# A graph-attention and mixture-of-experts kernel: dense edge stage on chip from counted node pairs

## The chip, the cores and the metric

The kernel runs on one core of one Trainium2 chip. The metric is the device time of one execution in microseconds, here the median of three runs.

## What is computed

x has 2500 nodes of 512 features, and 40000 edges (src, dst) come sorted by dst. Everything is fp32.

```python
h = layernorm(x) @ W + b_w
e = leaky_relu((h @ a[:512])[dst] + (h @ a[512:])[src] + b_a, 0.2)
w = exp(e)
alpha = w / segment_sum(w, dst)[dst]
x = x + segment_sum(alpha[:, None] * h[src], dst)
n = layernorm(x)
probs = softmax(n @ Wg + bg)
x = x + sum over the top 2 of 8 experts of probs_e * (gelu(n @ W1[e] + b1[e]) @ W2[e] + b2[e])
```

Since the weight of an edge depends on its two nodes alone, edges that join the same pair have the same weight.

## The kernel before, in words

The nodes lie in NT = 20 tiles of 128, the edges in 313 chunks of 128, four chunks to a group (GC = 4), 79 groups.

**Node rows.** For a pair of tiles u, ACT rounds the transposed x (`high_xT`, L867), POOL takes the rest (L496), PE multiplies the two halves with the two halves of the centred W (`products`, L645, 12 products a tile), DVE scales, adds the bias and takes the two dot products with a (`node_rows`, L1089, L1096), ACT turns these into scores (`scores`, L885, L888) and SP stores the rows in `node_table` in DRAM (L394). `ps_d` (L678) spreads the scores of the destinations along the free axis.

**Edges.** POOL gathers one row per edge from `node_table` with an indirect DMA per chunk (`gather`, L508) into a ring of eight groups. For each group ACT makes both exponentials of the leaky relu against a window of 128 destinations (`weights`, L915); DVE takes the larger (`largest`, L1150) and masks it with the edge's destination (`masked`, L1162); PE multiplies the result with the rows (`sums`, L686); DVE adds the sums into `acc` for the window (`add`, L1171). A word per group says where its window lies and whether it needs further ones (`extras`). POOL's order is the gathers' order; DVE's is mask of group g, then add of group g-2.

**Second normalisation and logits**, after the last group: for a pair of tiles DVE divides, adds x (`x1_of`, L1274) and takes statistics (L1280, L1287), ACT the root and the normalised rows (L951, L961), PE transposes (`normal_T`, L727), multiplies with Wg (`logits`, L736) and turns back (`logits_of_nodes`, L743), ACT copies between (L969, L976). SP stores x and the normalised rows, then loads W2 and W1 (L442, L436).

**Routing and experts**: DVE ranks the items, with one-hots in bf16 (L1383 to L1417), PE counts (L785, L794), and tiles of 128 routed items go through the experts with a gather (L595) and an adding scatter (L604) each. The change leaves these alone but for the rows that count as valid.

## Time and profile before

| what | us |
|---|---|
| timed runs, median of 3 (lowest, highest) | 771.3 (770.13, 773.55) |
| the profiled execution, first to last instruction | 843.5 |
| its PE, DVE, ACT, POOL busy | 630.6, 456.8, 356.8, 478.4 |

The profiled execution is one execution; its own time is known as its span alone, and that is 72.2 us above the median of the timed runs. Busy time of PE counts its matmul records; an fp32 product leaves two records, one of fp32r or bf16 one.

### The profile page before, as it was taken

The numbers are of one execution on the slowest core, as the hardware profiler recorded it, in microseconds if no ns is written. First come the engines' busy times: TensorE is split into PE (matmuls) and PEld (weight loads), VectorE is DVE, ScalarE is ACT, GpSimd is POOL, SyncE is SP. The second block draws the span as 40 slices with busy tenths as digits, with TensorE's granted clock in tenths as the row PEclk, the third lists the DMA queues.
The fourth block names the chain that finished last, engine by engine and source line by source line (L and its number), as shares of the span: only waits on it lengthen the run. The fifth ranks groups of instructions, "written<-read, shape, count | busy, mean of one in ns | idle before, by whom it ended". The sixth has DMA issues, their size and how long they took to land.

```text
span 843.5 us, 13398 instructions
## 1 busy us (share of the span) xinstructions
PE 630.6 (75%) x2874; PEld 497.9 (59%) x2875; DVE 456.8 (54%) x1139; ACT 356.8 (42%) x956; POOL 478.4 (57%) x550
## 2 busy tenths in 40 slices
PE   4997335766676757766686667774988899999992
PEld 2886224655564646655565555662645787888881
DVE  3999224564555546645555655579758433333331
ACT  3232323343443434433443434335864444545551
POOL 4461775666665666656666566501104377777773
PEclk9999677989999998798979889995998999999997
DMA  9482675656666656666666666505897277777765
GB/s 310 154 286 103 179 211 146 194 166 178 186 177 174 187 168 189 175 183 167 185 184 182 169 179 189 164 2 188 306 352 285 66 136 133 137 135 134 138 117 71
DMA packets 59260, 147.26 MB, mean 175 GB/s; under 512 B 8965, under 2 KB 18437, under 8 KB 58968
## 3 DMA queue, kind: packets, MB, share of 16 engines
q0 software_dynamic: 35216, 106.84, 50.3%
q1 hardware_dynamic: 24008, 40.01, 13.7%
q8 instruction: 14, 0.23, 0.1%
q14 instruction: 22, 0.18, 0.1%
HBM read 118.46 MB, written 28.35 MB: 174 GB/s over the span
## 4 chain that ended last, share of the span: by engine, by line
PE 45%; DVE 21%; issue 14%; DVEq 7%; another core or an unknown queue 6%; DMA 3%; SPq 1%; ACT 1%; POOLq 0%; POOL 0%; ACTq 0%
PE ps L686 22%; PE ps L825 8%; PE ps L839 6%; DVE acc L1171 4%; DVE S L1162 4%; DVE Wt L1150 3%; DVE junk L1096 3%; PE ps L736 2%; PE ps L815 2%; DVE rows L1089 1%; DMA x_all<-in_x_dram 1%; DVEq L1202 1%; DVEq L1171 1%; PE ps L727 1%
## 5 line engine op out<-in xcount | busy, mean ns | idle before, releaser
L686 PE MATMUL ps<-rows,S 128*128 128x257 f32 x1252 | 325.9, 423 | 156.9 <-DVE acc L1171 107.1
L508 POOL DMA_INDIRECT rows<-node_table,srcT x313 | 298.4, 953 | 178.5 <-issue 86.7
L686 PEld LDWEIGHTS ps<-rows,S 128*128 128x128 f32 x1252 | 263.1, 214 | 219.5 <-issue 160.7
L915 ACT ACTIVATE E<-sdst_w,rows 128x128 f32 x313 | 100.1, 390 | 284.0 <-DVE Wt L1150 187.7
L1171 DVE TENSOR_TENSOR acc<-acc,ps 64x514 f32 x160 | 110.1, 688 | 147.8 <-PE ps L686 68.6
L1162 DVE SCALAR_TENSOR_TENSOR S<-ps,lane,Wt 128x128 f32<-128x128 f32 x313 | 88.2, 345 | 26.3 <-issue 13.9
L915 ACT ACTIVATE ps<-sdst_w,rows 128x128 f32 x313 | 96.0, 350 | 0.0
L825 PE MATMUL ps<-W_e,xgT 128*128 x352 | 83.4, 380 | 0.0
L604 POOL DMA_INDIRECT out_dram<-y,si x44 | 70.4, 1601 | 12.1 <-issue 6.3
L825 PEld LDWEIGHTS ps<-W_e,xgT 128*128 128x128 f32 x352 | 63.4, 190 | 6.9
L645 PE MATMUL ps<-Wb,xT 128*128 128x512 f32 x240 | 56.5, 398 | 6.0 <-DVE Wb L1108 5.0
L839 PE MATMUL ps<-W_hi,hidT 128*128 x176 | 55.4, 437 | 3.8 <-DVE hidT L1452 3.7
L1469 DVE TENSOR_TENSOR y_b<-ps,b_b 128x512 f32<-128x512 f32 x44 | 30.4, 692 | 47.9 <-PE ps L839 36.8
L645 PEld LDWEIGHTS ps<-Wb,xT 128*128 128x128 f32 x240 | 46.0, 193 | 16.6 <-DVE Wb L1108 5.8
L1150 DVE SCALAR_TENSOR_TENSOR Wt<-E,ps 128x512 f32<-128x512 f32 (+1 forms) x79 | 53.0, 671 | 0.0
L595 POOL DMA_INDIRECT xg<-xn_table,gi x44 | 48.1, 1094 | 7.9 <-issue 5.1
L1022 ACT ACTIVATE act_h<-hid 128x256 f32<-128x256 f32 x44 | 18.4, 418 | 75.7 <-DVE hid L1459 66.9
L1459 DVE TENSOR_TENSOR hid<-ps,b_b 128x256 f32<-128x256 f32 x44 | 18.7, 424 | 51.1 <-PE ps L825 49.8
L496 POOL TENSOR_TENSOR xT<-xf,xT 128x1024 fp32r<-128x1024 f32 x10 | 26.2, 2616 | 29.0 <-ACT xT L867 29.0
L1155 DVE TENSOR_TENSOR lane<-dstT,base 128x4 f32 (+1 forms) x79 | 12.8, 162 | 54.4 <-issue 51.4
L553 POOL COPY si<-dst_row 128x1 int32 (+1 forms) x45 | 31.0, 689 | 18.9 <-DVE need L1443 11.3
L839 PEld LDWEIGHTS ps<-W_hi,hidT 128*128 128x128 f32 x176 | 32.5, 189 | 13.3 <-issue 7.7
(202 smaller groups left out, 612.9 us busy)
## 6 DMA issues: line engine op xcount, KB each, us to landing
W_e<-in_L_ffn_W_dram SPq DMA_DIRECT2D x16, 512.0 KB, 8.9
node_table<-rows SPq DMA_DIRECT2D x20, 258.0 KB, 3.2
xf<-in_x_cols_dram SPq DMA_DIRECT2D x10, 512.0 KB, 6.1
out_dram<-acc SPq DMA_DIRECT2D x20, 256.0 KB, 2.6
xn_table<-xn SPq DMA_DIRECT2D x20, 256.0 KB, 2.4
rows<-node_table,srcT POOLq DMA_INDIRECT x313
x_all<-in_x_dram SPq DMA_DIRECT2D x19, 256.0 KB, 6.6
b_b<-in_L_ffn_b_dram SPq DMA_DIRECT2D x1, 2048.0 KB, 14.6
```

The costliest lines, as they stand in the source:

```text
L508: nc.gpsimd.indirect_dma_start(out=rows[:, g % RING, c, :], out_offset=None, in_=table, in_offset=bass.IndirectOffsetOnAxis(ap=srcT[:, GC ...
L553: nc.gpsimd.tensor_copy(si[:, r, :], dst_row[:, bass.ds(i, 1)]).then_inc(si_ok, 1)
L595: nc.gpsimd.indirect_dma_start(out=xg[:, r, :], out_offset=None, in_=xn_table, in_offset=bass.IndirectOffsetOnAxis(ap=gi[:, r, :], axis=0) ...
L604: nc.gpsimd.indirect_dma_start(out=result, out_offset=bass.IndirectOffsetOnAxis(ap=si[:, (r - LAG) % YR, :], axis=0), in_=y[:, (r - LAG) % ...
L645: m = pe.matmul(ps_h[s][j][:, :], xT[:, s, a, k, j * P:(j + 1) * P], Wb[:, b, k, :], start=(n == 0), stop=(n == 3 * KT - 1))
L686: m = pe.matmul(ps_agg[q][:, a, 0:HALF], S[:, w, c, :], rows[:, r, c, a * HALF:(a + 1) * HALF], start=(c == 0), stop=(c == n - 1))
L825: m = pe.matmul(ps_hid[1 - s][:, 0:F], xgT[:, 1 - s, k * P:(k + 1) * P], W1_e[:, bass.ds(e, 1), k, :].rearrange("p e f -> p (e f)"), start ...
L839: m = pe.matmul(ps_y[s][:, :], hidT[:, s, a, k * P:(k + 1) * P], W[:, bass.ds(e, 1), k, :].rearrange("p e d -> p (e d)"), start=(c == 0), ...
L915: m = nc.scalar.activation(e[:, c, :], sdst_w[:, bass.ds(w, 1), :].rearrange("p w n -> p (w n)"), ACT.Exp, bias=bias, scale=scale)
L1150: return nc.vector.scalar_tensor_tensor(out=Wt[:, q, 0:n, :], in0=E1[:, q, 0:n, :], scalar=FINITE, in1=(E2x[:, 0, 0:n, :] if q == 2 else p ...
L1162: m = nc.vector.scalar_tensor_tensor(out=S[:, k, c, :], in0=ps_id[:, bass.ds(turn_of, P)], scalar=lane[:, k, c:c + 1], in1=Wt[:, q, c, :], ...
L1171: m = nc.vector.tensor_tensor(a, a, ps_agg[q][part, :, 0:HALF], ALU.add)
```

## The change

The tiles now hold TN = 125 nodes each (20 x 125 = 2500), padded to 128 rows. The rows h stay on chip, as a rounded half `H_hi` and the rest `H_lo`; `node_table` and all its gathers go. For a tile t of destinations the kernel counts how many edges join each pair of source and destination: the source is written as (tile k, place), and for ten half banks of 250 columns (12.5 destinations by 20 source tiles) PE multiplies a one-hot of the sources' places (`hot_l`) with a one-hot of (destination, source tile) (`hot_k`), both bf16, three chunks of edges for each half. A table of words says at which chunk each half begins; where three chunks do not do, a loop of extras follows. ACT makes the weight of every pair of the tile (20 relus and 20 exponentials of 128 x 125, one for each source tile), DVE multiplies it with the counts (`weigh`), sums it over the source tiles as a tree (`fold`), and splits it; PE multiplies it with H in three terms (hi hi, hi lo, lo hi), 60 products of 512 columns. x plus the sum, its statistics, the root (by POOL, in Newton steps from a seed), the normalised rows, their transposes and the logits are made inside the same loop, one to three tiles behind.

```diff
-    table = nc.dram_tensor("node_table", [NTN, ROW], F32).ap()
-            def gather(g):
-...
-                    nc.gpsimd.indirect_dma_start(
-                        out=rows[:, g % RING, c, :], out_offset=None, in_=table,
-                        in_offset=bass.IndirectOffsetOnAxis(ap=srcT[:, GC * g + c:GC * g + c + 1], axis=0))\
+        def over_node_tiles(eng, step, first=-1):
+
+            for t in range(first, 4):
+                step(t, t % 2)
+            with eng.Fori(2, NT // 2 - 1) as i:
+                for s in range(2):
+                    step(2 * i + s, s)
+            for t in range(NT - 2, NT + 3):
+                step(t, t % 2)
# POOL
+            def low_rows(u, s):
+                for j in range(2):
+                    pool.wait_ge(H_hi_ok, 2 * u + j + 1)
+...
+                    nc.gpsimd.tensor_tensor(H_lo[:, 2 * u + j, :], hrow[:, s, j, :],
+                                            H_hi[:, 2 * u + j, :].bitcast(F32), ALU.subtract).then_inc(H_lo_ok, 1)
+            def rstd_of_tile(t, s):
+...
+                after(nc.gpsimd.tensor_scalar(low, v, -0.5, None, ALU.mult), 1)
+                for n in range(3):
+                    after(nc.gpsimd.tensor_scalar(part, y, y, low, ALU.mult, ALU.mult), 2 * n + 2)
+                    if n < 2:
+                        after(nc.gpsimd.tensor_scalar(y, part, 1.5, y, ALU.add, ALU.mult), 2 * n + 3)
# PE
+            def count(t):
+...
+                if not (isinstance(t, int) and t < 1):
+                    pe.wait_ge(A_ok, t)
+                for h in range(HALVES):
+                    pe.wait_ge(pairs_ok, HALVES * t + h + 1)
+                    for c in range(BASE - h % 2):
+                        pe.matmul(half_of(h), low_of(h, c), hot_k[:, BASE * h + c, :],
+                                  start=(h % 2 == 0 and c == 0), stop=False)
+...
+            def tile_products(t, s):
+
+                if has(t, -1):
+                    count(t + 1)
+                if has(t, 0):
+                    if not (isinstance(t, int) and t < 1):
+                        pe.wait_ge(x1_ok, t)
+                    for k in range(NT):
+                        if k % (NT // 4) == 0:
+                            pe.wait_ge(A_hi_ok, 4 * t + k // (NT // 4) + 1)
+                        pe.matmul(ps_agg[0:TN, :], A_hi[:, k, :], H_hi[:, k, :], start=(k == 0), stop=False)
+                        m = pe.matmul(ps_agg[0:TN, :], A_hi[:, k, :], H_lo[:, k, :], start=False, stop=False)
+...
+                    for k in range(NT):
+                        if k % (NT // 4) == 0:
+                            pe.wait_ge(A_lo_ok, 4 * t + k // (NT // 4) + 1)
+                        m = pe.matmul(ps_agg[0:TN, :], A_lo[:, k, :], H_hi[:, k, :], start=False, stop=(k == NT - 1))
+                        if k == NT // 4 and has(t, 3):
+                            pe.wait_ge(den_ok, t + 1)
+                            logits_of_nodes(t - 3)
+                        if k == NT // 2 and has(t, 2):
+                            normal_T(t - 2, s)
+                    m.then_inc(agg_ok, 1)
# ACT
+            def tile_weights(t, s):
+
+                if has(t, 3):
+                    xnT_of(t - 3)
+                if has(t, 2):
+                    xn_of(t - 2, s)
+                if has(t, -2):
+                    relus(t + 2, s)
+                if has(t, -1):
+                    for q in range(2):
+                        high_weights(t + 1, 1 - s, q)
+                if has(t, 3):
+                    logT_of(t - 3)
+                if has(t, -2):
+                    exps(t + 2, s, 0)
+                if has(t, -1):
+                    for q in range(2, 4):
+                        high_weights(t + 1, 1 - s, q)
+                if has(t, -2):
+                    exps(t + 2, s, 1)
# DVE
+            def pair_rows(at):
+
+                shape = [P, SPAN, P // 2, 2]
+                return nc.vector.tensor_tensor(
+                    hot_l[:, 0:SPAN, :].rearrange("p c (n j) -> p c n j", j=2),
+                    lane_l[:, :].rearrange("p (n j) -> p n j", j=2).unsqueeze(1).to_broadcast(shape),
+                    lo2[:, bass.ds(at, SPAN), :].unsqueeze(2).to_broadcast(shape), ALU.is_equal)
+            def hot(into, h, key):
+
+                return nc.vector.tensor_scalar(into, lane_k[:, :], float(HW * h), key, ALU.add, ALU.is_equal)
+            def pairs_of(t, at, halves):
+
+                for h in halves:
+                    rel = dve.snap(within(dve.snap(regs[1 + h]), 0, SPAN - BASE))
+                    for c in range(BASE):
+                        m = hot(hot_k[:, BASE * h + c, :], h, key_t[:, bass.ds(rel + c, 1)])
+                    m.then_inc(pairs_ok, 1)
+            def weigh(t, s, b):
+...
+                m = nc.vector.scalar_tensor_tensor(out=some, in0=some, scalar=FINITE,
+                                                   in1=ps_count[b][:, 0:BC].rearrange("p (n k) -> p k n", k=NT),
+                                                   op0=ALU.min, op1=ALU.mult)
+            def tile_step(t, s):
+
+                here, ahead, behind = has(t, 0), has(t, -1), has(t, 1)
+                if behind:
+                    add_x(t - 1, 1 - s)
+                for q in range(4):
+                    if behind:
+                        await_variance(t - 1, q)
+                    if here:
+                        low_weights(t, s, q)
+...
+                    if behind:
+                        variance(t - 1, 1 - s, q)
+                at = None
+                if ahead:
+                    weigh(t + 1, 1 - s, 0)
+                if behind:
+                    variance(t - 1, 1 - s, 4)
+                if ahead:
+                    for b in range(1, BANKS):
+                        weigh(t + 1, 1 - s, b)
+                    fold(t + 1, 1 - s, 0)
+                    if has(t, -2):
+                        at = pair_keys(t + 2)
+                    fold(t + 1, 1 - s, 1)
+                    if has(t, -2):
+                        pair_rows(at)
+                    for n in range(2, 5):
+                        fold(t + 1, 1 - s, n)
+                if has(t, -2):
+...
+                    pairs_of(t + 2, at, range(0, HALVES // 2))
+                if here:
+                    reciprocal_of(t, s)
+                if has(t, -2):
+                    pairs_of(t + 2, at, range(HALVES // 2, HALVES))
```

In the stage of the node rows ACT also rounds each row (`high_rows`), DVE makes the edges' keys (`edge_keys`, seven operations on 128 x 320 and some small ones, after u = 1), finds the chunks of each half bank (`chunk_thresholds` and `chunks_of_halves`, four compares and four reductions of 128 x 384, after u = 2) and builds the table (`chunk_table`, after u = 7); the dot products are taken from PSUM, with a product by `rstd` for each pair of tiles behind them. Wg and bg are loaded at the start. ACT's queue holds `relus(0)` and `exps(0)` ahead of the loop.

## Rows read from the trace of the kernel before

**Rows 1.** stretches: length, busy PE, PEld, DVE, ACT, POOL, clock, DMA share, GB/s

```profile
40.00:80.00 40.00, 36.38 (x166) 30.04 (x165) 39.01 (x106) 10.27 (x31) 18.47 (x10) 0.98 0.61 206
...
85.00:566.00 481.00, 325.56 (x1252) 263.06 (x1252) 253.42 (x630) 189.34 (x628) 298.37 (x313) 0.87 0.61 172
...
720.00:760.00 40.00, 39.62 (x206) 33.10 (x204) 15.09 (x31) 20.78 (x42) 30.96 (x42) 1.00 0.74 133
```

**Rows 2.** groups: count | busy us, mean ns | idle before, its end

```profile
L686 PE MATMUL ps<-rows,S 128*128 128x257 f32 x1252 | 325.9, 423 | 156.9 <-DVE acc L1171 107.1
...
L508 POOL DMA_INDIRECT rows<-node_table,srcT x313 | 298.4, 953 | 178.5 <-issue 86.7
...
L915 ACT ACTIVATE E<-sdst_w,rows 128x128 f32 x313 | 100.1, 390 | 284.0 <-DVE Wt L1150 187.7
...
L1162 DVE SCALAR_TENSOR_TENSOR S<-ps,lane,Wt 128x128 f32<-128x128 f32 x313 | 88.2, 345 | 26.3 <-issue 13.9
```

**Rows 3.** timeline, POOL, edge stage: start, us, instruction, [idle before]

```profile
85.55 1.25 POOL L508 DMA_INDIRECT rows<-node_table,srcT  x1 [18.26 <-DMA node_table<-rows]
...
301.70 0.95 POOL L508 DMA_INDIRECT rows<-node_table,srcT  x1 [0.30 <-issue]
```

**Rows 4.** timeline, end of the edge stage and of the logits, PE and SP

```profile
549.96 16.37 PE L686 MATMUL ps<-rows,S 128*128 128x257 f32 x68 [3.23 <-DVE acc L1171]
...
612.95 5.92 SPq L442 DMA_DIRECT2D W_e<-in_L_ffn_W_dram  x8
...
616.09 1.23 PE L743 MATMUL ps<-ident,logT 8*128 8x8 f32 x8
```

**Rows 5.** timeline, PE: node rows' products, node logits, transposes, bf16 counts

```profile
39.70 8.55 PE L645 MATMUL ps<-Wb,xT 128*128 128x512 f32 x37
...
587.20 1.09 PE L727 MATMUL ps<-ident,xn 128*128 128x128 f32 x8
...
590.05 0.61 PE L743 MATMUL ps<-ident,logT 8*128 8x8 f32 x4
...
648.01 1.19 PE L794 MATMUL ps<-hot_p,hot_r 128*128 128x47 bf16 x40
```

**Rows 6.** timeline, DVE: setup, edge stage, second normalisation, routing

```profile
14.41 2.49 DVE L1108 TENSOR_TENSOR Wb<-Wf,Wb 128x512 fp32r<-128x512 f32 x4
...
300.22 1.13 DVE L1162 SCALAR_TENSOR_TENSOR S<-ps,lane,Wt 128x128 f32<-128x128 f32 x4 [0.24 <-issue]
...
588.42 1.41 DVE L1274 SCALAR_TENSOR_TENSOR acc<-acc,rden,x_all  x2 [0.42 <-issue]
...
627.92 0.49 DVE L1369 TENSOR_TENSOR rank<-rank,per 128x320 f32<-128x320 f32 x1
...
628.45 0.49 DVE L1371 TENSOR_TENSOR rank<-rank,choice 128x320 f32<-128x320 f32 x1
...
633.06 0.71 DVE L1385 TENSOR_SCALAR hot_v<-hot_t,part 128x1880 bf16<-128x1880 bf16 x1
...
633.69 2.11 DVE L1386 TENSOR_TENSOR hot_v<-hot_t,first_b 128x1880 bf16<-128x1880 bf16 x1
```

**Rows 7.** timeline, ACT: copies and table load ahead of the edges, exponentials

```profile
81.31 2.03 ACT L906 ACTIVATE sdst_w<-ps 128x512 f32<-128x512 f32 x4
...
84.21 1.28 ACT L939 ACT_TABLE_LOAD   x1
...
300.17 1.28 ACT L915 ACTIVATE E<-sdst_w,rows 128x128 f32 x4 [6.92 <-issue]
```

**Rows 8.** timeline, node rows: DVE's wait, POOL's part of a pair, DVE's last dot

```profile
22.07 1.28 DVE L1117 TENSOR_REDUCE group_mm<-dst_g 79x1 f32<-79x512 f32 x2 [3.59 <-DMA dstT<-in_dst_dram]
...
41.78 2.62 POOL L496 TENSOR_TENSOR xT<-xf,xT 128x1024 fp32r<-128x1024 f32 x1 [2.03 <-ACT xT L867]
...
80.02 0.69 DVE L1096 CUSTOM_DVE_ANT_0 junk<-rows,a_b 128x512 f32<-128x512 f32 x1
```

**Rows 9.** timeline, POOL, where it waits for its own copy

```profile
643.65 1.05 POOL L595 DMA_INDIRECT xg<-xn_table,gi  x1 [0.28 <-POOL gi L550]
```

More of the change, by code:

```diff
@@ L75, in gnn_moe_kernel @@
         spare = sb("spare", [P, 3], F32)
+        seed = sb("seed", [P, 2, 4], F32)
+        half = sb("half", [P, 2], I32)
+        xn2 = sb("xn2", [P, 2, D], F32)
+        xnT = sb("xnT", [P, KT, P], F32)
+        logT = sb("logT", [NX, P], F32)
+        Wg_sb = sb("Wg_sb", [P, KT, NX], F32)
+        bg_c = sb("bg_c", [NX, 1], F32)
         start = sb("start", [P, 5], F32)
@@ new lines, in normal_T, with logits @@
+            def normal_T(t, s):
+                pe.wait_ge(xn2_ok, t + 1)
+                if not (isinstance(t, int) and t < 1):
+                    pe.wait_ge(logT_ok, t)
+                for k in range(KT):
+                    m = pe.transpose(ps_T[:, k * P:(k + 1) * P], xn2[:, s, k * P:(k + 1) * P], ident[:, :])
+                m.then_inc(xnT_ps, 1)
+            def logits(t):
+                pe.wait_ge(xnT_ok, t + 1)
+                for k in range(KT):
+                    m = pe.matmul(ps_T[0:NX, 0:P], Wg_sb[:, k, :], xnT[:, k, :], start=(k == 0), stop=(k == KT - 1))
+                m.then_inc(logT_ps, 1)
@@ L909, in weights @@
-            def weights(q, r, w, n=GC):
-                low = E2x[:, 0, :, :] if q == 2 else ps_E2
-                for k, (e, scale) in enumerate(((E1[:, q, :, :], 1.0), (low, SLOPE))):
-                    for c in range(n):
-                        bias = rows[:, r, c, S_SRC + k:S_SRC + k + 1]
-                        m = nc.scalar.activation(e[:, c, :], sdst_w[:, bass.ds(w, 1), :].rearrange("p w n -> p (w n)"), ACT.Exp,
-                                                 bias=bias, scale=scale)
-                return m
@@ L936, in _ @@
-            act.wait_ge(odd_ok, 2)
-            act.wait_ge(win_ok, 2)
-            act.wait_ge(cst_ok, 1)
-            nc.scalar.activation(spare[:, 2:3], cst2[:, 0:1], ACT.Exp)
-            with act.Fori(0, NG // RING) as i:
-                window_words(act, regs, i)
-                for r in range(RING):
-                    group(r, i)
-            window_words(act, regs, NG // RING)
-            for r in range(NG % RING):
-                group(r, NG // RING, GC if r < NG % RING - 1 else GC_LAST)
@@ L992, in _, with relus @@
-            std2_of(0, 0)
-            over_steps(act, route_step)
+                n = min(4, NT - 4 * b) * TN
+                nc.scalar.activation(sdst_b[:, 4 * b * TN:4 * b * TN + n], ps_d[b][:, 0:n], ACT.Copy).then_inc(d_ok, 1)
+            def relus(t, s):
+                if not (isinstance(t, int) and t < 2):
+                    act.wait_ge(A_lo_ok, 4 * t - 4)
+                    act.wait_ge(sum_ok, t - 1)
+                dst_scores = sdst_b[:, bass.ds(t * TN, TN)]
+                for k in range(NT):
+                    m = nc.scalar.activation(weight[:, s, k, :], dst_scores, ACT.Relu, bias=ss[:, 0, k:k + 1],
+                                             scale=1.0 - SLOPE)
+                    if k % (NT // 2) == NT // 2 - 1:
+                        m.then_inc(relu_ok, 1)
@@ new lines, in exps, with high_weights @@
+            def exps(t, s, part):
+                act.wait_ge(relu_ok, 2 * t + part + 1)
+                for k in range(part * NT // 2, (part + 1) * NT // 2):
+                    m = nc.scalar.activation(weight[:, s, k, :], weight[:, s, k, :], ACT.Exp, bias=ss[:, 1, k:k + 1])
+                if part == 1:
+                    m.then_inc(exp_ok, 1)
+            def high_weights(t, s, q):
+                if q == 0:
+                    act.wait_ge(A_ok, t + 1)
+                if not (isinstance(t, int) and t < 1):
+                    act.wait_ge(hi_ps, 4 * t - 4 + q + 1)
+                some = slice(q * NT // 4, (q + 1) * NT // 4)
+                nc.scalar.activation(A_hi[:, some, :], weight[:, s, some, :], ACT.Copy).then_inc(A_hi_ok, 1)
@@ L994, in _ @@
+            act.wait_ge(d_ok, len(ps_d))
+            act.wait_ge(s_ok, NT // 2)
+            act.wait_ge(ld_late, 16 * 2)
+            relus(0, 0)
+            for part in range(2):
+                exps(0, 0, part)
+            act.wait_ge(H_lo_ok, NT)
+            over_node_tiles(act, tile_weights)
             act.wait_ge(shift_ok, 1)
@@ L1122, in step @@
+            def step(u, s, ahead):
                 rstd_of(u, s)
```

991 lines of the change are left out of this document (484 added, 507 removed).

## The prediction

> **What bounds the kernel now.** The first gather of the edge stage starts at 85.55 [rows 3], its last matmuls end at 566.3, and the last logits of the second normalisation at 617.3 [rows 4]; behind these come routing and experts, to 843.5 us. So I read the table by stretches along these bounds first [rows 1]. The edges take over half of the span, and no engine is full there: PE is busy 325.6 of 481 us, POOL 298.4, DVE 253.4, ACT 189.3.
>
> The groups of instructions [rows 2] name the work: 313 gathers on POOL and 1252 matmul records on PE, with exponentials on ACT and mask and add on DVE. POOL's timeline shows a gather every 1.25 us (0.95 and 0.30 of issue) [rows 3]: 313 of them are 392 us, a floor under the edge stage. The stage takes 480.8 us, 6.1 us for each of 79 groups against 5.0 at POOL's pace. What ended each group's idle time [rows 2] shows the rest as a ring of hand-overs: ACT waits 187.7 us for DVE's `Wt`, PE 107.1 for DVE's add.
>
> The timed runs' median is 771.3 us, 72.2 below the profiled span. I put this excess into the edge stage: 480.8 less 72.2 is 408.6, just above POOL's floor, while setup (DVE 39.0 of 40 us) and experts (PE 39.6 of 40) have no such room [rows 1]. All sums below are made in the profiled execution's times, and their total is read as a timed result, since the new kernel has no gather left in its edges. The danger of that reading is among the cases. About 0.5% (3.9 us) is what a measurement can tell here from no change.
>
> **The new loop, per tile of 125 nodes.** There are 20 tiles.
>
> PE. Sixty products of 512 columns: 37 like them took 8.55 us, which is 0.226 each once the last one's 0.4 is taken off [rows 5]; 13.6 us. Thirty counting products of 250 bf16 columns: below, 40 of 47 columns took 1.19 us, 0.030 each; above, 0.226. By columns in between it is 0.116; 3.5 us (ends 0.9 and 6.8). Four transposes, 8 records in 1.09 us [rows 5]: 1.0. Four logit products of 128 columns, as wide as the transposes: 1.0. Denominator and node logits, 4 records at 0.15 [rows 5]: 0.6. PE: 19.7 us.
>
> DVE. The durations overlap a little, so I use the distance from start to start [rows 6]: 0.60 for 512 fp32 elements (four in 2.49, last 0.69), thus 0.07 beside the elements; 0.66 with a scalar pointer and PSUM; 0.63 for 1880 bf16 elements with a pointer, which is four elements per element time of the fp32 row, and 0.14 beside them; 0.53 for 320 elements where each waits for the one before, 0.20 beside them. Then: `add_x` 0.67. Four low parts of 625: 0.72 each, 2.9. Statistics 0.6, and four small ones 0.5. Five weighings of 500 from PSUM at 0.65: 3.3 (read there with a stride of 20, which no row shows; below 3.3 nothing speaks for it, above, double). The tree of 1250, 625, 250, 125 and 125 with waits: 3.2. Keys 0.15, reciprocal with its waits 0.4. The source one-hots at once, 2304 bf16 elements: between 0.8 (the pointer form's pace) and 2.5 (the tensor-by-tensor form, 2.11 for 1880 [rows 6]); I take 2.5, the same operation. The 30 pair one-hots, 250 elements each with a pointer: 0.065 and 0.135, so 0.20, 6.0 in all. Ends: 0.145 (the smallest overhead) and 0.39 (one element at a time): 4.4 and 11.7. DVE: 20.2 us.
>
> The Trainium skill, "VectorE: DVE Perf Modes", "The perf-mode tier table", gives `tensor_tensor` in bf16 twice the fp32 pace where every innermost step is one; the stored rows have a step of zero there and do not show it. The new code copies each value into two neighbours, so by that rule the source one-hots take 1.3 us, DVE falls to 19.0 and PE sets the pace.
>
> ACT. Forty activations of 125: four of 128 take 1.28 us [rows 7] and one about 0.39 [rows 2], so 0.295 each, 11.8. Four copies of 625, by columns from 0.51 for 512 [rows 7]: 0.62, 2.5. `xnT`, `xn` and `logT`, from 0.4 to 0.8: 1.7. ACT: 16.0 us, hidden under the other two; without that cover a tile cannot be shorter than this. POOL has eight linked one-element steps, about 3 us, hidden too.
>
> The order within a tile lets these run side by side. PE counts tile t+1 while DVE adds x of t-1 and makes the low weights of t, which PE wants only after its 40 high products; DVE's weighing waits for the counts (3.5 us in), behind 5 us of its own work; the exponentials are a whole step early. One barrier is left per step: `add_x` waits for the last product, 0.2 us. So a step takes the longer of PE and DVE: **T = 20.4 us**. No engine waits for a gather any more and PE is never idle for long, so I take the upper level of its clock, 2.4 GHz, throughout (the edge stage now has 0.87 of it, the stretch that the 0.226 is from 0.98 [rows 1]).
>
> **Before the loop.** Today DVE ends the last node row at 80.6 and the broadcast scores are copied by 84.2, where ACT goes on to its table load [rows 7, 8]. Added to DVE's queue, which is full there: one product with `rstd` per pair, 0.35 with its wait, 3.5 for ten; edge keys, seven operations of 320 at 0.49 [rows 6] and small ones, 4.0; thresholds 1.3; four spans of 384 and their reductions, 1.1 together, 4.4; the chunk table, ten linked ones at 0.25, 2.5. The bias dots (2 us) fit into the 3.6 us that DVE waits for `dstT` [rows 8]. POOL's halves go from 2.6 us per pair [rows 8] to 5.3, against PE's 24 products at 0.226, 5.4: hidden, just. The table stores and POOL's wait of 18.3 us for them [rows 3] go. Scores ready: 84.2 + 15.7 = 99.9.
>
> Then nothing covers anything: relus 5.9, table load 1.3 [rows 7], exps 5.9, relus of tile 1 5.9 (queued ahead of the high weights; DVE's first weighing, 3.3, hides under them), two quarters of the high part 1.2, half the next exps 3.0, the other two 1.2, 20 high and 20 low products 9.0. Tile 0 ends at 133.5 (99.9 and 33.6).
>
> **After the loop.** The second normalisation's 51 us go; what is left is one tile's way through: add, statistics, seed 2.2, POOL's steps 3.2 (eight of 0.1, with up to 0.28 of hand-over as between its copy and its gather [rows 9]), `xn` 0.8, transposes, copy, logits, copy, nodes 3.5, hand-overs 1.2: 10.9 us. Loading the expert weights starts about 4 us ahead of the last logit, as now (612.95 against 617.3 [rows 4]); POOL's constants, some 20 small fills, fit under the tail. From there on nothing changes: 843.5 - 617.3 = 226.2.
>
> **Sum**: 133.5 + 19 x 20.4 + 10.9 + 226.2 = **758.2 us**, 13 below the median. Each 1 us of T is worth 19; at T = 21.1 there is no gain.
>
> **The rivals.**
> *PE alone sets the pace, and the excess was not all in the edges.* The one-hots at double pace give T = 19.7, 745 us; if the profile also stretched the other stages by up to its mean 8.6%, the 336 us beside the loop shrink by as much as 29, to about 716. For it: nothing shows where the excess lies, and the one-hots' layout differs from the stored rows'. Against: those stages are full. 0.23. The page's rule named above would bring the double pace about.
> *The hand-overs cost as they do now.* The groups now take 6.1 us where the busiest engine needs 5.0; the new step has far fewer barriers for its length, but 3% of it (0.7 us) gives T = 21.1: 771 us, no change. 0.12.
> *The pair one-hots bound the loop: slower.* Thirty small DVE instructions, each with a column address from a register, stand on the engine that is already the longest. `masked`, with a pointer and 128 elements, shows 0.262 from start to start (1.13 less the last one's 0.345, by three) [rows 2, 6]. At that price T is 22.3 and the time 794; at 0.30, 23.4 and 815; at one element at a time, 26.1 and 867. It decides above 0.22 us. For it: the 0.24 of issue ahead of `masked`'s first, where registers are worked out [rows 6]. Against: those 0.262 hold 0.133 of elements that four at a time shrink to 0.065. 0.25.
> *The change does not do what it says.* A tile where a half bank spans over three chunks takes the extra loop, ten linked rounds of about 0.9 us: 9 us a tile, up to 938 us. A half holds 12.5 nodes, 200 edges, 1.6 chunks, and of the reference's own sorted indices none spans four: 0.03. Setup held up by POOL or code loading beyond 15 us: slower as well, 0.03.
>
> **Chances.** Forecast 0.34 (748 to 767), first rival 0.23, no change 0.12, slower 0.31. Faster 0.57. The range 720 to 822 leaves out the pair one-hots at full price and the extra loop.
>
> **What would show it.** Right: no indirect DMA ahead of the experts, steps of 20 to 21 us, DVE and PE over 90% busy, clock near 1.0, pair one-hots 0.20 us apart, scores ready near 100 us, last logit near 532. Wrong: PE waiting for `hot_k` or `A_lo` in each step, the 2304-element compare well under 2.5 us, gaps of issue on DVE between pair one-hots, or the experts' stage shorter than 192 us.

## The result: slower, 788.0 us, and the profile after

The changed kernel takes 788.0 us (median of 4 runs, 786.6 to 788.7) against 770.7 for the kernel before in the same session: ratio 1.022, 95% interval 1.019 to 1.025. The forecast was 758, faster; the time lies in the range, the sign is wrong.

The profiled execution of after spans 786.0 us and took 787.7 as timed: here nothing lies between profile and runs, so its rows can be set against the sum directly. First the stretches (length, busy time of PE, PEld, DVE, ACT and POOL with counts, granted clock, DMA share, GB/s): setup, first tile, the steady steps, and what follows.

```profile
0.00:109.00 109.00, 78.45 (x304) 60.69 (x305) 92.47 (x230) 36.91 (x81) 51.52 (x44) 0.87 0.33 118
109.00:152.00 43.00, 27.29 (x125) 17.57 (x126) 36.31 (x117) 40.22 (x126) 0.00 (x0) 0.80 0.01 2
152.00:540.00 388.00, 379.94 (x1920) 278.04 (x1918) 329.26 (x958) 270.60 (x808) 87.53 (x169) 1.00 0.07 26
540.00:566.00 26.00, 17.78 (x83) 12.09 (x81) 6.52 (x27) 6.70 (x12) 7.54 (x37) 0.82 0.39 125
566.00:596.00 30.00, 25.92 (x209) 15.21 (x207) 27.05 (x49) 16.85 (x25) 8.18 (x6) 0.87 0.94 356
596.00:786.00 190.00, 172.10 (x930) 143.38 (x925) 67.70 (x141) 87.49 (x176) 128.73 (x173) 0.97 0.69 119
```

The edge stage has lost its gathers and its hand-overs: PE is busy 379.9 of 388 us at full clock, where [rows 1] had 325.6 of 481 at 0.87. PE sets the pace. DVE is idle for 59 us in that stretch. What DVE waits for is seen in the waits of 152 to 540 (total us, times, longest), DVE first, then PE:

```profile
DVE x_all L1353 <- PE ps L790: 39.4, 15, 9.1
DVE hot_k L1278 <- DVE weight_sum L1327: 3.9, 17, 0.2
```

```profile
PE ps L737 <- issue: 5.5, 16, 0.5
PE ps L759 <- DVE den L1345: 1.5, 1, 1.5
```

One step, PE's timeline from one tile's counts to the next (start, length, instruction, idle before). Rows of the high products are left out:

```profile
151.75 2.88 PE L726 MATMUL ps<-hot_k,hot_l 128*128 128x250 bf16 x25
...
322.06 0.86 PE L737 MATMUL ps<-hot_k,hot_l 128*128 128x250 bf16 x5 [0.32 <-issue]
...
333.53 1.56 PE L790 MATMUL ps<-H_hi,A_lo 128*125 128x512 f32 x6
335.02 0.38 PE L759 MATMUL ps<-ident,logT 8*128 8x8 f32 x2
...
339.11 4.33 PE L726 MATMUL ps<-hot_k,hot_l 128*128 128x250 bf16 x25
343.76 0.82 PE L737 MATMUL ps<-hot_k,hot_l 128*128 128x250 bf16 x5 [0.31 <-issue]
```

339.11 less 317.85, where the step's own counts began, is 21.3 us; the step behind is 21.7. From DVE's `add_x` (L1353) at 210.54 to that at 490.13 there are 13 steps: **21.5 us each**, forecast 20.4. "Issue" is time in which an engine waits for nothing that the profile shows. The 25 counting products take 4.33 us and the five behind them 0.82 with 0.3 of issue ahead of them: 5.3 us until the next product starts (4.9 in the step before). Yet the row at 151.75, from the straight code ahead of the loop, has the same 25 in 2.88, the 0.115 each that the prediction worked out.

DVE in the same step:

```profile
318.23 0.75 DVE L1353 SCALAR_TENSOR_TENSOR x_all<-ps,rden,x_all 125x512 f32 x1 [1.66 <-PE ps L790]
...
323.69 2.42 DVE L1311 SCALAR_TENSOR_TENSOR weight<-weight,ps 128x500 f32<-128x500 f32 x4
326.14 1.46 DVE L1321 TENSOR_TENSOR tree<-weight 128x1250 f32<-128x1250 f32 x1
...
328.40 1.34 DVE L1271 TENSOR_TENSOR hot_l<-lane_l,lo 128x2304 bf16<-128x2304 bf16 x1
...
330.95 3.02 DVE L1278 TENSOR_SCALAR hot_k<-lane_k,key_t 128x250 bf16<-128x250 bf16 x15 [0.23 <-DVE weight_sum L1327]
333.89 0.15 DVE L1345 TENSOR_SCALAR den<-ps 125x1 f32<-125x1 f32 x1
...
334.20 3.02 DVE L1278 TENSOR_SCALAR hot_k<-lane_k,key_t 128x250 bf16<-128x250 bf16 x15
340.13 0.75 DVE L1353 SCALAR_TENSOR_TENSOR x_all<-ps,rden,x_all 125x512 f32 x1 [2.90 <-PE ps L790]
```

The 2304-element one-hots take 1.35 us and 15 pair one-hots 3.02, 0.2 apart.

The start. First DVE in the setup and at the first tile, then POOL in the setup, PE at the first tile, and ACT where the scores are ready:

```profile
37.55 2.41 DVE L1182 CAST lane_l<-lane_i 128x128 bf16<-128x128 int32 x1
...
47.87 1.99 DVE L1150 TENSOR_TENSOR s_dot<-s_raw,rstd 128x4 f32<-128x4 f32 x1
...
88.86 2.31 DVE L1225 TENSOR_SCALAR rel_n<-rel_n 1x200 f32<-1x200 f32 x1
...
122.21 3.02 DVE L1311 SCALAR_TENSOR_TENSOR weight<-weight,ps 128x500 f32<-128x500 f32 x5 [4.43 <-ACT weight L982]
...
130.05 5.93 DVE L1278 TENSOR_SCALAR hot_k<-lane_k,key_t 128x250 bf16<-128x250 bf16 x30 [0.22 <-DVE weight_sum L1327]
```

```profile
37.37 2.50 POOL L501 TENSOR_TENSOR xT<-xf,xT 128x1024 fp32r<-128x1024 f32 x1
...
47.50 2.34 POOL L501 TENSOR_TENSOR xT<-xf,xT 128x1024 fp32r<-128x1024 f32 x1
...
88.57 2.48 POOL L501 TENSOR_TENSOR xT<-xf,xT 128x1024 fp32r<-128x1024 f32 x1
```

```profile
130.98 5.79 PE L726 MATMUL ps<-hot_k,hot_l 128*128 128x250 bf16 x25 [11.41 <-DVE hot_k L1278]
```

```profile
109.01 5.90 ACT L973 ACTIVATE weight<-sdst_b,ss 128x125 f32<-128x125 f32 x20
```

Against the terms of the sum:

| term | forecast | measured | miss |
|---|---|---|---|
| scores ready | 99.9 | 109.0 | +9.1 |
| to the end of tile 0's products | 33.6 | 42.7 (to 151.75) | +9.1 |
| 19 further tiles | 387.6 | 397.3 (to 549.0; 20.9 each, the first and last ones shorter) | +9.7 |
| tail of the normalisation | 10.9 | 12.8 (to 561.8) | +1.9 |
| routing and experts | 226.2 | 224.2 | -2.0 |

Together +27.8, 786.0 us.

### The profile page after: what moved, and what is told of

Same layout as the page of the kernel before. It is cut to its first block, busy times and chain, and to the rows that moved or that the text cites. A ratio compares the mean times of both kernels' runs of the same rounds, so it can differ in the third digit from the quotient of the medians.

```text
span 786.0 us, 15439 instructions
## 1 busy us (share of the span) xinstructions
PE 701.5 (89%) x3556; PEld 527.0 (67%) x3557; DVE 559.3 (71%) x1520; ACT 458.8 (58%) x1226; POOL 283.5 (36%) x427
## 4 chain that ended last, share of the span: by engine, by line
PE 52%; DMA 10%; issue 5%; DVE 4%; POOL 2%; POOLq 2%; ACT 0%; DVEq 0%; ACTq 0%
PE ps L772 10%; PE ps L790 10%; PE ps L773 9%; DMA out_dram<-y,si 9%; PE ps L726 7%; PE ps L879 3%; PE ps L753 2%; PE ps L893 2%; PE ps L737 2%; PE ps L820 1%; DMA xg<-xn_table,gi 1%; PE ps L746 1%; PE ps L869 1%; PE ps L759 1%; DVE hot_r L1509 1%
## 5 line engine op out<-in xcount | busy, mean ns | idle before, releaser
L973 ACT ACTIVATE weight<-sdst_b,ss 128x125 f32 (+1 forms) x400 | 118.3, 386 | 95.5 <-DVE A_lo L1339 95.5
L772 PE MATMUL ps<-H_hi,A_hi 128*125 128x512 f32 x400 | 163.0, 408 | 0.9 <-DVE x_all L1353 0.9
L773 PE MATMUL ps<-H_lo,A_hi 128*125 128x512 f32 x400 | 157.9, 395 | 0.0
L1278 DVE TENSOR_SCALAR hot_k<-lane_k,key_t 128x250 bf16<-128x250 bf16 x600 | 120.6, 282 | 4.4 <-DVE weight_sum L1327 4.3
L982 ACT ACTIVATE weight<-weight,ss 128x125 f32<-128x125 f32 x400 | 119.8, 384 | 0.0
L790 PE MATMUL ps<-H_hi,A_lo 128*125 128x512 f32 x400 | 104.9, 402 | 0.0
L726 PE MATMUL ps<-hot_k,hot_l 128*128 128x250 bf16 x500 | 80.7, 286 | 16.0 <-DVE hot_k L1278 15.9
L772 PEld LDWEIGHTS ps<-H_hi,A_hi 128*125 128x125 f32 x400 | 74.2, 185 | 21.6 <-issue 3.7
L773 PEld LDWEIGHTS ps<-H_lo,A_hi 128*125 128x125 f32 x400 | 74.3, 186 | 16.1
L790 PEld LDWEIGHTS ps<-H_hi,A_lo 128*125 128x125 f32 x400 | 71.4, 185 | 15.9
```

The source lines that it names most:

```text
L726: pe.matmul(half_of(h), low_of(h, c), hot_k[:, BASE * h + c, :], start=(h % 2 == 0 and c == 0), stop=False)
L772: pe.matmul(ps_agg[0:TN, :], A_hi[:, k, :], H_hi[:, k, :], start=(k == 0), stop=False)
L773: m = pe.matmul(ps_agg[0:TN, :], A_hi[:, k, :], H_lo[:, k, :], start=False, stop=False)
L790: m = pe.matmul(ps_agg[0:TN, :], A_lo[:, k, :], H_hi[:, k, :], start=False, stop=(k == NT - 1))
L973: m = nc.scalar.activation(weight[:, s, k, :], dst_scores, ACT.Relu, bias=ss[:, 0, k:k + 1], scale=1.0 - SLOPE)
L982: m = nc.scalar.activation(weight[:, s, k, :], weight[:, s, k, :], ACT.Exp, bias=ss[:, 1, k:k + 1])
```

## The experiments

Every ratio is to the kernel before in the run's own session, where its median was 770.0 to 772.3 us; so a difference of under some 2 us between runs of different sessions says nothing by itself.

Theory A at the outset: the counting products are slow for the registers in their addresses, and PE's step follows. Its rivals were the wait for the denominator and DVE's instructions.

**e1_static_low.** Fixed addresses; the counts are then of the wrong chunks.

```diff
-                    return hot_l[:, bass.ds(chunk[h] + c, 1), :].rearrange("p c n -> p (c n)")
+                    return hot_l[:, h + c, :]
```

> The left operand of each counting product is taken at a fixed place of hot_l (h + c) and not at one from a register; so a half bank may meet the wrong chunk of sources, and the sums are not the reference's. Theory A: in the loop PE's count takes 5.3 us and not 3.5 because its instructions wait for their register addresses; then it falls to about 3.6 us, the step from 21.5 to about 19.8 and the time from 788 to about 760 (757 to 766). Theory B (a bf16 product of 250 columns costs 0.155 us in itself in this loop): count, step and time stay, 785 to 791. Theory C (DVE or a barrier sets the step): count shorter, step and time unchanged.

Measured: 793.5 us, ratio to before 1.028 [1.024, 1.031]; 5.5 us above after, 3.9 once the shift of the kernel before between the sessions is taken off. Of the forecasts theory C is the nearest: the count is shorter, but the step did not stay, it grew. PE's timeline says why:

```profile
314.57 0.38 PE L759 MATMUL ps<-ident,logT 8*128 8x8 f32 x2 [2.60 <-DVE den L1345]
314.88 2.11 PE L790 MATMUL ps<-H_hi,A_lo 128*125 128x512 f32 x5
...
317.50 2.90 PE L790 MATMUL ps<-H_hi,A_lo 128*125 128x512 f32 x9
320.25 2.88 PE L726 MATMUL ps<-hot_k,hot_l 128*128 128x250 bf16 x25
322.97 0.70 PE L737 MATMUL ps<-hot_k,hot_l 128*128 128x250 bf16 x5
```

The stretch behind that wait, in the columns of the first table:

```profile
300.00:310.00 10.00, 10.00 (x49) 7.68 (x48) 9.41 (x17) 6.37 (x21) 4.34 (x7) 1.00 0.14 53
314.50:317.50 3.00, 2.93 (x11) 2.36 (x12) 3.00 (x16) 3.00 (x11) 0.00 (x0) 0.64 0.00 0
```

The counts did shrink, to 2.88 and 0.70 with no issue: 1.9 us less. But PE now waits for `den` ahead of the node logits, 24.7 us in 15 waits over 152 to 540: 2.60 here, 0.69 in the step before. Behind the long wait the granted clock is 0.64, the full 2.4 GHz for a part of the stretch and 1.2 for the rest: five products take 2.11 where after has 1.41. From count to count PE's steps are 20.3 and 23.8 us in turn, and the two effects give back more than the 1.9 (step 22.1 us, as the mean over ten). So the cost was where theory A put it, and the gain was not to be had by that edit alone.

**e2_recip_early.** The reciprocal, which frees the bank that the node logits share, ahead of all pair one-hots.

```diff
-                    pairs_of(t + 2, at, range(0, HALVES // 2))
                 if here:
                     reciprocal_of(t, s)
                 if has(t, -2):
-                    pairs_of(t + 2, at, range(HALVES // 2, HALVES))
+                    pairs_of(t + 2, at, range(HALVES))
```

> DVE takes the denominators ahead of all thirty pair one-hots and not between the halves, so den_ok comes some 3 us earlier. PE has a wait for it five products into its low part, and behind that wait stand the last fifteen products and the next count. Theory A, in the form that PE's queue stands still at that wait and so works out the count's addresses too late: count falls from 5.3 to about 3.8 us, step to about 20, time to 760 to 768. Theory A without that (addresses cost their time wherever they stand): no change, 785 to 791. Theory B: no change either.

Measured: 786.3 us, 1.019 [1.016, 1.022], a step 21.5 as in after: no change. By itself the wait for `den` costs after nothing (1.5 us in the whole stretch, in the waits above).

**e3_pad_pairs.** Ten more small compares on DVE, one behind each half's pair one-hots, into a spare row.

```diff
                     m.then_inc(pairs_ok, 1)
+                    nc.vector.tensor_scalar(hot_k[:, HALVES * BASE, 24 * h:24 * h + 24], lane_k[:, 0:24], float(HW * h),
+                                            key_t[:, bass.ds(rel, 1)], ALU.add, ALU.is_equal)
```

> DVE makes ten more small compares per tile (24 columns each, at about 0.14 us, 1.4 us per tile) into a place that nothing reads. PE sets the step (DVE waits 2.9 us for the last product in each): time within 3 us of 788. DVE sets it, as the prediction had it: step +1.4, time about 815.

Measured: 803.6 us, 1.042 [1.038, 1.045], halfway between the two forecasts. DVE stood idle for 1.4 to 3.1 us ahead of each `add_x` in after, and 1.4 us more work (DVE's first steps are 20.0 us here, 18.65 in after) still cost 15 us. PE's waits over 152 to 540 in this run:

```profile
PE ps L759 <- DVE den L1347: 12.9, 9, 2.5
```

Half of the added work stands ahead of the reciprocal, and PE waits there as in e1. But the slow steps, every second one, are DVE's own: from its `add_x` at 374.20 to that at 397.23 it works 20.0 us and stands 2.85 more with nothing to wait for (issue), while the last product had ended by 394.9. The idle time of after was not all slack; e6 shows what it is.

**The theory that came of these, A2.** A step has two limits close together. PE's own work in after is 21.5 us. The other is a ring: last product, `add_x` (318.23), low weights, weighing, tree, half the pair one-hots, `den` (333.89), 15.8 us on DVE; then PE's node logits and its last 14 products and transposes, 4.5. That is 20.5. By this theory removing either limit alone gains 1 us at best, or loses, since PE idles and its clock falls.

**e4_dots_one_input.** In the setup, the dots times `rstd` as four one-element products with a pointer in place of one with two tensors from SBUF.

```diff
-                nc.vector.tensor_tensor(s_dot[:, s, :, :], s_raw[:, s, :, :],
-                                        rstd[:, s, :].unsqueeze(1).to_broadcast([P, 2, 2]), ALU.mult).then_inc(dot_ok, 1)
+                for k in range(2):
+                    for j in range(2):
+                        m = nc.vector.tensor_scalar(s_dot[:, s, k, j:j + 1], s_raw[:, s, k, j:j + 1], rstd[:, s, j:j + 1],
+                                                    None, ALU.mult)
+                m.then_inc(dot_ok, 1)
```

> The product of the dots with rstd, one instruction with two inputs in SBUF per pair of tiles (1.1 us on average, up to 2.0), becomes four of one element with a pointer scalar. Theory D: DVE cannot start an instruction with two SBUF inputs while POOL's own runs, and waits for its end; then these take some 0.35 us together, scores are ready at about 101 and not 109 us, and the time falls by 6 to 9 us to about 780. Rival (the long ones wait for the dots before them, or DVE's queue is full whatever the form): scores ready within 2 us of 109, time 786 to 790.

In after the group of the dots is (count, busy us, mean ns, idle before):

```profile
L1150 DVE TENSOR_TENSOR s_dot<-s_raw,rstd 128x4 f32<-128x4 f32 x10 | 11.3, 1135 | 0.3
```

Measured: 786.8 us, 1.020 [1.017, 1.022]. The group of the dots falls from 11.3 us to 5.8 and the scores are ready at 106.4, 2.6 us earlier; the end gains 1.2 at most, too little to tell from none. The time is as the rival said (786 to 790), the scores lie between its forecast (107 or later) and theory D's (101), nearer to its own. Timelines of DVE and of POOL in this run:

```profile
47.42 0.58 DVE L1152 TENSOR_SCALAR s_dot<-s_raw,rstd 128x1 f32<-128x1 f32 x4
47.92 1.69 DVE L1199 TENSOR_SCALAR chunk<-chunk_i 128x384 f32<-128x384 int32 x1
```

```profile
47.05 2.34 POOL L501 TENSOR_TENSOR xT<-xf,xT 128x1024 fp32r<-128x1024 f32 x1
```

The dots no longer wait. But the next instruction does: a compare of 384 int32 that takes 0.35 us in after takes 1.69, and it ends 0.2 us behind POOL's subtraction. This is what one expects if the wait belongs to POOL's running instruction and passes to the next DVE instruction of the kind that it holds up. Seen here are the four products that are not held up and one compare that is.

**e6_static_recip.** e1 and e2 together.

> Both edits of the first two runs at once: fixed addresses for the stationary source one-hots (so the sums are of the wrong chunks: that part of the computation is changed) and the reciprocal ahead of all pair one-hots. Theory A2: two limits lie close together in a step. PE's own work is 21.5 us, 1.9 of it because each counting product follows a register instruction; and a ring through DVE is 20.5: last product, add, low weights, weighing, tree, half the pair one-hots, denominator (15.8 us on DVE), then PE's node logits and its last 14 low products (4.5). Either edit alone leaves the other limit, and where the ring binds PE idles and its clock falls. With both, a step is PE's 19.6 us, the ring 17.5, DVE's busy time 18.6: about 1.9 us off each of some 17 steps, 755 us (750 to 762), DVE waiting 0.5 to 1 us for the last product, no wait of PE for the denominator, clock near 1.0 in the loop. Rival B2 (DVE's own queue, or something else that the first two runs did not touch, sets the pace and both edits are beside the point): 784 or more.

Measured: 762.1 us, 0.989 [0.985, 0.992]: 26 us under after, where the two edits apart gave +5.5 and -1.7. This is at the upper end of A2's range and 22 us below B2's. From `add_x` to `add_x` the steps are 19.2 and 20.6 to 20.9 us in turn, 19.9 as a mean, not 19.6: one tile in each turn of the loop is longer. 0.3 us in each of the loop's 14 tiles is 4 of the 7 us above the expected 755; the rest is not traced. What makes that tile longer stands in the rows, DVE's and then PE's:

```profile
358.85 5.94 DVE L1278 TENSOR_SCALAR hot_k<-lane_k,key_t 128x250 bf16<-128x250 bf16 x30
366.87 0.75 DVE L1353 SCALAR_TENSOR_TENSOR x_all<-ps,rden,x_all 125x512 f32 x1 [2.08 <-issue]
```

```profile
363.85 2.88 PE L726 MATMUL ps<-hot_k,hot_l 128*128 128x250 bf16 x25
...
367.75 0.49 PE L772 MATMUL ps<-H_hi,A_hi 128*125 128x512 f32 x1 [0.49 <-DVE x_all L1353]
```

The product that `add_x` needs ended at 364.0, yet it starts at 366.87, 2.1 us behind the last pair one-hot, and PE, whose count is now short, waits for it. Such a pause comes once in each turn of the loop (issue ahead of `add_x`: 12.2 us in six turns here, 17.4 in e1, 17.3 in e3) and in no step of straight code (e7, e8, e10). A2 had overlooked this **third limit**: DVE's own queue, 18.65 us of work and 1.9 to 3.1 of pause in every second tile, about 21.5 in after, as long as PE's step. It sets the slow steps of e3 and e6, and in e1 it delays `add_x`, so that the ring's wait of 2.60 falls in the step behind it. In the code only the loop's turn stands there; what in it takes the time is not shown.

**e7_unrolled_recip.** Straight code for all tiles, with e2's edit. Nothing of the computation changes.

```diff
-            for t in range(first, 4):
-                step(t, t % 2)
-            with eng.Fori(2, NT // 2 - 1) as i:
-                for s in range(2):
-                    step(2 * i + s, s)
-            for t in range(NT - 2, NT + 3):
+            for t in range(first, NT + 3):
                 step(t, t % 2)
```

> The reciprocal ahead of all pair one-hots, and all tiles written out in straight code on each engine in place of the loop of two; nothing of the computation changed. In the changed kernel's own trace the counting products of the tiles ahead of the loop take 2.9 to 3.0 us for 25 and those inside it 3.9 to 4.4, with 0.3 of issue behind them. Theory A2 (register work inside the loop: sums for the waits beside the addresses): 25 products take 2.9 to 3.0 in all tiles, a step is 20.0 us, the time 762 (757 to 768). Rival C (straight code must be fetched; the early tiles were short only because PE waited there anyway): steps of 21 us or more, gaps of issue on PE or DVE, 780 to 800.

Measured: 771.3 us, 1.000 [0.998, 1.001], 17 us under after. PE's timeline, one tile:

```profile
311.49 2.91 PE L721 MATMUL ps<-hot_k,hot_l 128*128 128x250 bf16 x25
314.71 0.85 PE L732 MATMUL ps<-hot_k,hot_l 128*128 128x250 bf16 x5 [0.31 <-issue]
```

The 25 products take 2.9 to 3.1 in every tile and a step 20.35 us (13 steps from 230.26 to 494.80). Theory C falls, since the steps are under 21 us and no new gap of issue appears; but the time lies above A2's range (757 to 768) too. Of A2 the counts are right and the step was put 0.35 too short.

**e8_unrolled.** Straight code alone.

> Straight code alone, the reciprocal left between the halves of the pair one-hots. Theory A2: PE could do a step in 20.0 us but the ring through the denominator takes 20.5 and PE idles in front of the node logits: 1 us or less off each step at best, with a clock that dips: 772 to 786. If the ring is not real, this run equals the one with the reciprocal moved too (762 by A2).

Measured: 773.4 us, 1.002 [0.999, 1.004], at the lower end of what A2 allowed; a step is 20.4. The ring of 20.5 and PE's own 20.35 are too near for this run to part them: in its profile PE waits for `den` once between 200 and 480, for 1.5 us. So nothing here shows the ring bind in straight code. That PE waits for `den` in the loop rests on e1 and e3.

**e10_straight_static.** e7 with fixed addresses.

> Straight code and the reciprocal moved, and fixed addresses for the source one-hots besides (the counts are then of the wrong chunks, as in the first run). It parts the two costs of the loop of two tiles: with fixed addresses inside the loop a step was 19.5 and 20.3 us in turn. Theory A2 (0.7 us per turn of the loop are its branch, 0.8 us a step in straight code are the 30 addresses): all steps 19.5 to 19.6 us, 756 to 759. Rival G (addresses cost nothing in straight code, where 25 products take 2.9 to 3.0 us with them as without, and PE's 20.35 us has another cause): 768 or more.

Measured: 757.8 us, 0.984 [0.979, 0.988], all steps 19.5 (246.12 to 480.16 are 12 of them), PE without a wait and busy 347.2 of 348 us:

```profile
152.00:500.00 348.00, 347.20 (x1875) 271.59 (x1872) 323.29 (x944) 269.43 (x805) 86.51 (x162) 1.00 0.07 28
```

So G falls. A step of PE with fixed addresses is 19.5; the register addresses add 0.85 in straight code (0.3 of it the issue ahead of the last five). With them the loop adds 1.15 more (21.5 against 20.35), all of it in PE's count; why the same addresses cost more there is not shown. Without them it adds 0.4 (e6, 19.9), and that is not PE's: it is the wait for DVE's `add_x` at the loop's turn.

**e9_straight_best.** e7, e4, and tile 1's keys and source one-hots while DVE waits for the first exponentials.

```diff
+                opening = isinstance(t, int) and t == -1
+                if opening:
+                    dve.wait_ge(bank_ok, 1)
+                    at = pair_keys(1)
+                    pair_rows(at)
                 if ahead:
                     weigh(t + 1, 1 - s, 0)
...
-                    if has(t, -2):
+                    if has(t, -2) and not opening:
                         at = pair_keys(t + 2)
                     fold(t + 1, 1 - s, 1)
-                    if has(t, -2):
+                    if has(t, -2) and not opening:
                         pair_rows(at)
```

> A version meant to beat both kernels, nothing of the computation changed: straight code for all tiles, the reciprocal ahead of the pair one-hots, the dots as one-element products with a pointer (scores 2.6 us earlier in the run of before with that edit alone, 1.3 us of it left at the end), and tile 1's keys and source one-hots made before the first weighing, in the 4.4 us in which DVE waits for the first exponentials (1.6 us off DVE's chain at the start). Theory A2 (straight code 771.3, then terms that add): 768 to 770, 0.3% under before. Rival: the early gains are lost again once PE sets the pace (PE's 20.35 us a step do not care when DVE starts): 770 to 772.

Measured over 12 runs: 766.8 us against 770.0, ratio 0.995 [0.993, 0.997], 1 us better than A2's 768 to 770. It beats both kernels, the one before by 0.5%. `add_x` of tile 0 starts at 149.49, where after has 153.02 (scores at 106.7), and against e7 the ratio falls by 0.5%, so the early gains are kept.

**e5_before_half.** The kernel before with 19,584 edges; the others are left out.

```diff
-    edges = laid["src"].shape[0]
+    edges = 19584
-    src_p[0:edges], dst_p[0:edges] = laid["src"], laid["dst"]
+    src_p[0:edges], dst_p[0:edges] = laid["src"][0:edges], laid["dst"][0:edges]
```

> The kernel before with half its edges (19,584 of 40,000 with the node count's own: 39 groups in place of 79; the other edges are left out, everything else as it was). It measures where the profiled execution of before, 72 us longer than the median of its runs, is longer. Theory E (the excess is in the edge stage, as the prediction took it): a group costs 5.0 to 5.2 us in the timed runs, so this run is 200 to 208 us shorter than before, 563 to 571 us, while its own profile shows 6.1 us per group and an excess of about half. Rival F (the profile stretches everything alike, or the excess lies elsewhere): 6.1 us per group in the timed runs as well, 244 us shorter, 527 us, and an excess that stays near 72.

Measured: 615.9 us, 0.799 [0.795, 0.803], outside both forecasts: 156 us less, not 200 or 244. The profiles tell more. The first row is this run's gathers over the stage, the other two are POOL's waits in the kernel before:

```profile
L508 POOL DMA_INDIRECT rows<-node_table,srcT x153: 952/957/1152, 87.6 to 279.4; - x153
```

```profile
POOL rows L508 <- remote: 40.2, 17, 5.1
POOL rows L508 <- PE ps L686: 33.3, 17, 2.7
```

The 153 gathers run from 87.6 to 279.4, 1.26 us apart without a wait but issue, 5.0 a group; the span is 615.4, as long as the run. In the kernel before, POOL's two kinds of waits hold 73.5 us, and the profile is 72.2 above the runs. With the waits gone, the excess is gone as well. That speaks for E. What put the time off is the drain: 58.9 us from the last gather (279.4) to the last product (338.3), against 22.8 (543.2 and 566.0) in the kernel before. PE's timeline shows what fills it:

```profile
293.73 1.13 PE L686 MATMUL ps<-rows,S 128*128 128x257 f32 x4 [0.69 <-DVE S L1162]
...
336.88 2.08 PE L686 MATMUL ps<-rows,S 128*128 128x257 f32 x4 [2.93 <-DVE S L1162]
```

There are ten such rounds, one after the other, and they are the experiment's own doing. The last group is filled up with edges of destination 4095, which counts as the last node; here the real edges end near the middle of the nodes, so that group spans ten further windows (652 records against 4 x 153, where the kernel before has 1252, just 4 x 313). The rounds last from 293.7 to 339.0. Without these 45 us the run would take about 571, an estimate, the upper end of E's 563 to 571. Whether the timed runs of before have exactly no such waits of POOL stays open.

## Why the prediction was wrong, step by step

**Right.** PE, not POOL, bounds the edges; no gather ahead of the experts; clock 1.00 in the loop. Pair one-hots 0.20 us apart (forecast 0.20), so the rival that put the slower side there is out: it named the wrong engine. Weighing with its stride 0.59 from start to start (forecast 0.65), ACT hidden (270.6 busy of 388), experts unchanged, POOL's Newton steps hidden but in the tail. That the excess of the profile of before lies in its edges fits e5, without being shown outright.

**The first rival's half.** The source one-hots take 1.35 us where I took 2.5, "the same operation". The Trainium skill, "VectorE: DVE Perf Modes", "The perf-mode tier table", had the double pace for `tensor_tensor` in bf16; the rows of before could not show it, and the trace of after agrees. It made DVE short (busy 329.3 of 388 us, 18.2 a step, where I had 20.2), and so PE set the pace as that rival said, with a longer step than its 19.7.

**The first step that failed: "Thirty counting products ... 3.5 us".** The price by columns is right for the product itself (2.88 for 25 with fixed addresses). From the first of the thirty to the next product it is 3.2 us with fixed addresses (e1, e6, e10), 3.9 to 4.1 with register addresses in straight code (e7), and 4.9 to 5.4 inside the loop. Each product takes its stationary operand at an address worked out from a register (`chunk[h] + c`), and that is what e1 and e10 take away; the profile does not list register instructions, so the reading rests on these edits. The range of 0.9 to 6.8 held it, but I had charged registers only to DVE, as the price of the pair one-hots, and not to PE, where the same change puts them. Of the step's other terms, the 40 high and 20 low products took 0.233 each where I had 0.226 (+0.4); the transposes 0.36 where I had 1.0. The forecast's 19.7 for PE was 1.8 short in all, and its 20.4 for the step, made for DVE, 1.1.

**The second: "One barrier is left per step".** There are two. The node logits wait for the denominator's bank to be read, and this stands behind the larger part of DVE's step. It costs after nearly nothing, but it decides what a saving on PE is worth (e1). The same sentence also put nothing for the turn of the loop, where DVE pauses 1.9 to 3.1 us (e6); that is hidden in after and is why e3's work on DVE cost so much.

**The third: "one product with `rstd` per pair, 0.35 with its wait".** It takes 1.14 as a mean over ten, 11.3 in place of 3.5. In the rows above DVE's `s_dot` at 47.87 has four elements, takes 1.99 and ends at 49.86; POOL's subtraction at 47.50 ends at 49.84. The cast at 37.55 stands so against POOL's at 37.37, and the table's one-partition operation at 88.86 against POOL's at 88.57, with ends within 0.15 us of each other. The Trainium skill, "SBUF — State Buffer", "Who interferes with whom", says that a DVE instruction with two SBUF inputs, or in a two-port mode, is shut out for the whole of a GpSimd instruction that reads SBUF and was issued first. The ends of these rows agree with it. The prediction priced POOL's added subtraction (2.5 us a pair) as hidden under PE, and not as something that DVE waits behind. e4 shows the wait to be moved, for a part, and not removed by changing one victim: 5.5 us less in the dots brought the scores 2.6 us forward. I did not try to change POOL's side, so how much of the 9.1 its waits hold is not shown.

**The fourth: "Then nothing covers anything".** I followed ACT from the scores to tile 0's products. DVE is busy, with no pause over 0.22 us, from 122.21 to its `add_x` at 153.02: weighing, tree, and then the counts' operands of tile 1 (130.05, 5.93 us), which PE wants ahead of tile 0's products, since `count(t + 1)` leads its step. PE waits 11.4 us for them and then works at the lower level of its clock (0.50 from 131 to 137, below; 25 products in 5.79 against 2.88). The lower level costs little, since DVE makes the last of these one-hots only at 136.0. All sixty products of the tile stand behind that count, from 137.48 to 151.75 (14.3 us), where the forecast had twenty of them done beside ACT's work and 9.0 us left: 5.3 of the 9.1. An order that is right in the steady state is paid for once at the start.

```profile
122.00:131.00 9.00, 0.02 (x1) 0.03 (x1) 8.47 (x17) 9.00 (x30) 0.00 (x0) 0.57 0.00 0
131.00:137.00 6.00, 5.91 (x26) 2.73 (x27) 6.00 (x28) 5.15 (x16) 0.00 (x0) 0.50 0.01 3
```

Two slips in the sums change nothing: the terms up to tile 0's end add up to 33.4, not 33.6, and 0.065 with the smallest overhead of 0.07 makes 4.1 us for the thirty pair one-hots, not 4.4.

Four misses of 9.1, 9.1, 9.7 and 1.9 us, all to the same side, outweigh the 13 that were forecast. Of the tail's 1.9, some 1.3 are its last transposes and logits: 1.11 and 1.87 us where a step inside the loop has 0.60 and 1.04, at a granted clock of 0.57 from 556 to 562. The chance of slower stood at 0.31, but for another reason; that the time still lies in the range is owed to the range's width, not to the mechanism.

## What to carry to other kernels

Price a register in an address on the engine that reads it: on PE it cost 0.85 us for 30 small products in straight code and 2.0 in a loop (21.5 against 19.5 a step). In a loop, read also what the turn itself costs on every engine; here DVE paused up to 3.1 us there, behind another engine's work that hid it. Before an engine's work is shortened, follow every wait of its step back through the other engines, not only the last one; where two limits lie within 1 us, only both edits together pay (+5.5 and -1.7 us apart, -26 together). And when work is put on POOL beside a full DVE, list which DVE instructions overlap it, the four-element ones too.

## What the runs showed of the hardware

- The same 25 products of 250 bf16 columns, each with an address worked out from a register, take 2.9 to 3.1 us in straight code (e7) and 3.9 to 4.4 inside a loop of two tiles (after); with fixed addresses 2.88 in either (e10, e1).
- At the turn of that loop DVE stands 1.9 to 3.1 us with nothing to wait for (e1, e3, e6); in straight code no such pause is seen (e7, e8, e10).
- Writing 20 tiles out in straight code on five engines brought no new gap of issue on PE (4.8 us in 14 between 200 and 480, all ahead of the last five counting products): e8 is 15 us faster than after by that alone.
- A wait of 2.6 us on an otherwise full PE is followed by a granted clock of 0.64 for 3 us (five products in 2.11 us against 1.41); over 300 to 540 it is 0.96 in e1 and 1.00 in after.
- DVE instructions of 4 to 384 elements took up to 2.4 us while POOL subtracted (1.99 and 2.41 in after, 1.69 in e4), each ending within 0.25 us of POOL's instruction.
- The compare of 2304 bf16 elements with pairwise copies takes 1.35 us (0.59 ns an element); the 250-element ones with a pointer follow each other at 0.20 us.
